# Transposes around a triangular inverse on VectorE, and head norms by one product on all rows, in a gated delta-rule layer on one core

## What is computed

```
q = l2norm(conv_silu(x Wq) + ramp * p20_q)          # the same for k; 16 heads of 16
v = conv_silu(x Wv) + ramp * p20_v
step: S = S * exp(g);  e = (v - S k) * beta;  S = S + k e^T;  o = S q * scale
reads = rmsnorm(o) over each head of 16
y = sigmoid(gate) * (concat(reads, normed_p20) @ out_W + out_b);  x1 = layernorm(x + y)
```

## Time and profile before

| what | value |
|---|---|
| median of three runs (lowest to highest) | 5939.71 us (5938.71 to 5969.02) |
| the profiled execution | 5967.04 us |
| its span, first to last instruction | 5965.4 us |
| mean granted clock of TensorE | 0.912 of full speed |
| TensorE busy in the span | 5158.8 us (86%) |
| VectorE busy | 2928.0 us (49%) |
| ScalarE busy | 1756.1 us (29%) |
| last router product of the first part starts (L1086) | 3435.3 us |

### The profile page before, as it was taken

The page is one execution under the profiler, slowest core; times in us unless marked ns, Lnnn a source line. Parts: engine busy times, 40 slices in busy tenths (PEclk is TensorE's granted clock), DMA queues, the critical chain, the costliest instruction groups (busy, mean ns, idle before and its releaser), DMA issues. The chain is left out here.

```text
span 5965.4 us, 218898 instructions
## 1 busy us (share of the span) xinstructions
PE 5158.8 (86%) x98967; PEld 3328.7 (56%) x98967; DVE 2928.0 (49%) x6701; ACT 1756.1 (29%) x2887; POOL 538.5 (9%) x657
## 2 busy tenths in 40 slices
PE   5999999999999999999999658999999999999400
PEld 3555565656656565656565535666666666666300
DVE  6667676767667676767676384000000001000255
ACT  3333333333333343434333101212212211211122
POOL 0000000000000000000000001111111111111376
PEclk9899899999999999999998679999999999999755
DMA  1000000000000000000000001111111111111365
GB/s 30 18 15 22 19 18 22 19 22 15 22 19 20 21 18 22 18 22 19 22 19 18 14 4 40 50 33 50 49 35 47 36 49 50 35 50 35 96 190 174
DMA packets 170008, 220.32 MB, mean 37 GB/s; under 512 B 32306, under 2 KB 148083, under 8 KB 169075
## 3 DMA queue, kind: packets, MB, share of 16 engines
q1 hardware_dynamic: 122994, 106.02, 5.6%
q0 software_dynamic: 29312, 84.97, 4.9%
q10 hardware_dynamic: 16896, 16.78, 0.8%
HBM read 138.50 MB, written 67.11 MB: 34 GB/s over the span
## 5 line engine op out<-in xcount | busy, mean ns | idle before, releaser
L1407 PE MATMUL bank<-gathered_T,w1s 128*128 128x512 f32 x2048 | 928.8, 613 | 67.6 <-DVE gathered_T L1350 67.6
L1418 PE MATMUL bank<-w2s,hidden_T 128*128 128x256 f32 x4096 | 894.6, 379 | 0.0
L1418 PEld LDWEIGHTS bank<-w2s,hidden_T 128*128 128x128 f32 x4096 | 775.7, 190 | 117.8 <-issue 15.3
L1377 ACT ACTIVATE hidden_T<-bank,b_expert 128x512 f32<-128x512 f32 x512 | 352.0, 687 | 1544.4 <-PE bank L1407 1544.4
L1407 PEld LDWEIGHTS bank<-gathered_T,w1s 128*128 128x128 f32 x2048 | 399.3, 196 | 559.5 <-issue 557.8
L1357 DVE TENSOR_TENSOR result_rows<-bank,b2s 128x512 f32<-128x512 f32 x128 | 88.6, 692 | 1217.7 <-PE bank L1418 1217.7
L900 PE MATMUL bank<-xT_and_z_out,ctrlW 128*128 128x512 f32 x768 | 383.9, 623 | 4.3 <-issue 4.3
L900 PE MATMUL bank<-np,p20W 128*128 128x512 f32 x768 | 375.3, 619 | 7.1 <-DVE conv_out L693 4.4
L1350 DVE COPY gathered_T<-bank 128x512 f32<-128x512 f32 x128 | 88.6, 692 | 557.8 <-PE bank L1396 541.9
L1136 POOL MEMSET tri<- 128x128 f32 x1 | 0.2, 209 | 3430.5 <-POOLq L337 3430.5
L1038 PEld LDWEIGHTS bank<-yb,bd_v 32*32 32x32 f32 x16384 | 188.7, 114 | 210.5 <-issue 209.9
(11 more groups left out here) (287 smaller groups left out, 7624.7 us busy)
## 6 DMA issues: line engine op xcount, KB each, us to landing
expert_rows<-result_rows SPq DMA_DIRECT2D x64, 512.0 KB, 2.9
x<-L_attn_hidden SPq DMA_DIRECT2D x33, 512.0 KB, 3.8
out_squares<-L_attn_hidden SPq DMA_DIRECT2D x32, 512.0 KB, 3.6
x_rows<-x SPq DMA_DIRECT2D x32, 512.0 KB, 3.1
x_rows_sb<-x_rows SPq DMA_DIRECT2D x32, 512.0 KB, 4.3
out<-out_rows ACTq DMA_DIRECT2D x32, 512.0 KB, 3.1
w1s<-L_ffn_w POOLq DMA_DIRECT2D x8, 1024.0 KB, 5.9
w2s<-L_ffn_w POOLq DMA_DIRECT2D x8, 1024.0 KB, 7.8
```

The costliest lines, as they stand in the source:

```text
L1377: nc.scalar.activation(hT[:, j, m, :], ring["h", j, m][:, :], ACT.Gelu, bias=b1e[:, par, m:m + 1]).then_inc(hT_ready, 1)
L1407: ins = nc.tensor.matmul(ps[:, :], w1s[:, par, k, m * P:(m + 1) * P], xgT[:, j, k, :], start=k == 0, stop=k == 1)
L1418: ins = nc.tensor.matmul(ps[:, i * D:(i + 1) * D], hT[:, j, m, s0:s0 + P], w2s[:, par, m, :], start=m == 0, stop=m == MT - 1)
```

## The change

**Norms.** A 128x128 matrix of ones in blocks of 16 (`hblk`) takes the place of the 128x32 sums and the 32-row spreading. One product a tile gives the head sum on all 128 rows, so ScalarE's logarithm and exponential work on all rows of each tile (into `sq4`, and `y1r` for the outputs), and VectorE scales from there. The tile `sq4` shares memory with `xT`; so the copy of the next `xT` waits for the last scaling (`kqi_ready`). The decay logits get a tile of their own (`dec_in`).

**Inverse.** VectorE transposes 32x32 blocks before and after the inverse, 512 columns an instruction, in place of TensorE and two PSUM banks. For this the first block of an eviction goes to a tile of its own, `a_rows`, with the token index outermost (an evicted group is now four VectorE instructions), and `X` has the column outermost. ScalarE reads the turned tile from SBUF.

**Order.** The four `ORDERS` strings are new. On SP's queue the log-row DMAs now stand behind the store of the unit's rows.

The diff, cut to its core:

```diff
-        X = FX[:, :].rearrange("p (h i c) -> p h i c", i=CHUNK, h=HPT // 2)
+        X = FX[:, :].rearrange("p (c b i) -> p b c i", i=CHUNK, b=4)
...
-        order += [(("nrm",), "act")] + [(("put", i), "dve") for i in range(4)]
+        order += [(("nrm", i), "act") for i in range(4)]
...
-        order += [(("aT", t), "act") for t in range(2)] + [(("T", t), "act") for t in range(2)]
...
-            pe=("CACBACCBBCCBABBABCABBABCABBACBBCCCACCACC" "ABBCACCCBBCBBACBBCBBAABBACBBAABCBAABCBAA"),
-            dve=("CBCAAACCABBABAAAABBABCBBAABCBBBBBCBBBBCB" "BBBCAABCBCCAAAAACABAAAACACACACBABBAAABBA" "AA"),
-            act=("BBACBBBBBCCAAAAAAAAABBCBABCCACCCCBBBAABB" "BACCAAACC"),
-            sp="AACC")
+            pe=("ACCABCCBCBBCBACBABBABCABBBACCACCCCACCAAC" "CACCCBBCBBABBABBABBABBACBBAABACABC"),
+            dve=("BCCAACAABCABBAAAABCBBBBAABBCABBBCABBCBBB" "CBBBABBBCBCCBBBAAAAAACAAAABBACACCAACAABB" "BAABAA"),
+            act=("BABABBCBCBCBAAACAABBAAACBCABCACCCCBBBABB" "AACABAACAACAC"),
+            sp="ACCA")
... ScalarE, streams A, B, C
+                    act.wait_ge(kqi_ready.sem, kqi_ready.before(u))
                     for e in range(2):
                         act.wait_ge(ra.filled, ra.full(u, ("xT", e)))
                         A(xT[:, e, :], ra["xT", e][:, :], ACT.Copy).then_inc(a_act, 1)
...
-                    A(rsn[:, :], ra["nrm",][:, :], ACT.Ln, scale=nsc[:, 0:1], bias=eps[:, 3:4]).then_inc(a_act, 1)
-                    A(rsn[:, :], rsn[:, :], ACT.Exp, scale=-0.5).then_inc(mrs_ready.sem, 1)
+                    for i in range(4):
+                        act.wait_ge(ra.filled, ra.full(u, ("nrm", i)))
+                        A(sq4[:, i, :], ra["nrm", i][:, :], ACT.Ln, scale=1.0 if i < 2 else float(HD),
+                          bias=eps[:, 0:1] if i < 2 else eps[:, 3:4]).then_inc(a_act, 1)
+                        for n in ((), (0,), (1,), (2, 3))[i]:
+                            act.wait_ge(a_act, ra.done(u, ("nrm", n)))
+                            A(sq4[:, n, :], sq4[:, n, :], ACT.Exp, scale=-0.5).then_inc(mrs_ready.sem, 1)
...
-                        A(X[:, :, 8 * t:8 * t + 8, :].rearrange("p h i c -> p i h c"), rb["aT", t][:, :].rearrange("p (i h c) -> p i h c", i=8, c=CHUNK),
-                          ACT.Copy, scale=-1.0).then_inc(b_act, 1)
+                        act.wait_ge(a_turned.sem, a_turned.of(u, t + 1))
+                        A(X[:, :, :, 8 * t:8 * t + 8], half(turned, t).rearrange("p (i b c) -> p b c i", b=4, c=CHUNK), ACT.Copy,
+                          scale=-1.0).then_inc(x_ready.sem, 1)
...
-                        ps = rb["T", t][:, :].rearrange("p (c g) -> p g c", g=G)
+                        act.wait_ge(t_turned.sem, t_turned.of(u, t + 1))
+                        ps = half(turned, t).rearrange("p (c g) -> p g c", g=G)
...
+                    for hh in range(2):
+                        act.wait_ge(rc.filled, rc.full(u, ("on", hh)))
+                        A(half(y1r, hh), rc["on", hh][:, :], ACT.Ln, scale=1.0 / HD, bias=eps[:, 0:1]).then_inc(c_act, 1)
+                    for hh in range(2):
+                        A(half(y1r, hh), half(y1r, hh), ACT.Exp, scale=-0.5).then_inc(ors_ready.sem, 1)
... VectorE
-                        V.tensor_tensor(apk[:, gs, 0:TILE].rearrange("p g (a i) -> p g a i", a=2), ps[:, :, 0:TILE].rearrange("p g (a i) -> p g a i", a=2),
-                                        F[:, gs, :].unsqueeze(2).broadcast_to([P, 8, 2, CHUNK]), ALU.mult)
+                        V.tensor_tensor(a_rows[:, :, gs].rearrange("p i g -> p g i"), ps[:, :, 0:CHUNK], F[:, gs, :], ALU.mult)
+                        V.tensor_tensor(apk[:, gs, 0:CHUNK], ps[:, :, CHUNK:TILE], F[:, gs, :], ALU.mult)
...
+                    for t in range(2):
+                        V.transpose(half(turned, t), a_rows[:, 8 * t:8 * t + 8, :].rearrange("p i g -> p (i g)")).then_inc(a_turned.sem, 1)
+                        yield
+                    dve.wait_ge(x_ready.sem, x_ready.of(u))
...
-                        sb_.then(V.tensor_tensor(X[:, :, j + 1:, 0:j], X[:, :, j + 1:, 0:j], t, ALU.add))
+                        sb_.then(V.tensor_tensor(X[:, :, 0:j, j + 1:], X[:, :, 0:j, j + 1:], t, ALU.add))
...
+                    for t in range(2):
+                        V.transpose(half(turned, t), half(FX, t)).then_inc(t_turned.sem, 1)
+                        yield
... TensorE
-                        ins = T.matmul(ps[PAIRS[i], :], hsum[:, :], sq4[:, i, :], start=True, stop=True)
-                        T.matmul(ps[:, :], hput[PAIRS[i], :], rsn[PAIRS[i], :], start=True, stop=True).then_inc(ra.filled, 1 + (ra.pads if i == 3 else 0))
+                        pe.wait_ge(msq_ready.sem, msq_ready.of(u, i + 1))
+                        ps = ra.take(pe, u, ("nrm", i))
+                        T.matmul(ps[:, :], hblk[:, :], sq4[:, i, :], start=True, stop=True).then_inc(ra.filled, 1 + (ra.pads if i == 3 else 0))
...
-                                ins = T.matmul(ps[r, j * G:(j + 1) * G], apk[r, :, 8 * t + j], ident[r, r], start=True, stop=True)
-                                ins = T.matmul(ps[r, j * G:(j + 1) * G], FX[r, 8 * t + j::CHUNK],
-                                               ident[r, r], start=True, stop=True)
...
+                        ps = rc.take(pe, u, ("on", hh))
+                        T.matmul(ps[:, :], hblk[:, :], half(osq, hh), start=True, stop=True).then_inc(rc.filled, 1)
```

More of the change, by code:

```diff
@@ L194, in attention @@
         FX = sb("fx", P, W2)
-        apk = sb("apk", P, G, 3 * CHUNK)
+        a_rows = sb("a_rows", P, CHUNK, G)
+        apk = sb("apk", P, G, TILE)
         bdkb = sb("bd_kb", P, G, TILE)
         tmp = sb("inverse_tmp", P, 4 * 56)
+        turned = sb("turned", P, W2)
         YB = sb("yb", P, G, TILE)
@@ L269, in attention, with ring @@
         MS = (2, 3, 0, 1, 4, 5)
-        def ring(r, order, at):
+        def ring(r, order, at, pads_by="act"):
             while len(order) % len(at):
-                order.append((("pad", len(order)), "act"))
+                order.append((("pad", len(order)), pads_by))
             return Bank(order, at, filled[r], {w: emptied[r, w] for w in ("act", "dve")})
@@ L283, in attention @@
         order += [(("mm1", t), "dve") for t in range(8)]
-        order += [(("aT", t), "act") for t in range(2)] + [(("T", t), "act") for t in range(2)]
         order += [(("Y", t), "act") for t in range(4)] + [(("M", t), "dve") for t in range(4)]
-        rb = ring("B", order, banks[3:6])
-        order = [(("L", c), "act") for c in range(NCH)] + [(("on",), "act")]
-        order += [(("put", hh), "dve") for hh in range(2)] + [(("proj", q), "dve") for q in range(2)]
+        rb = ring("B", order, banks[3:6], "dve")
+        order = [(("L", c), "act") for c in range(NCH)] + [(("on", hh), "act") for hh in range(2)]
+        order += [(("proj", q), "dve") for q in range(2)]
         order += [(("x1T", b), "act") for b in range(2)] + [(("lg",), "act")]
@@ L368, in c_ @@
                 def c_(u, k, grp, s):
-                    sp.wait_ge(rc.filled, rc.full(u, ("on",)))
+                    sp.wait_ge(rc.filled, rc.full(u, ("on", 1)))
                     rows(xres, grp, s, res_loaded.sem)
@@ L437, in a_ @@
                     yield
-                    act.wait_ge(a_dve, ra.done(u - 1, ("put", 3)))
+                    act.wait_ge(gl_ready.sem, gl_ready.before(u))
                     act.wait_ge(ra.filled, ra.full(u, ("dec",)))
@@ L769, in a_ @@
                     for i, m in enumerate(MS[0:4]):
-                        dve.wait_ge(ra.filled, ra.full(u, ("put", i)))
+                        dve.wait_ge(mrs_ready.sem, mrs_ready.of(u, i + 1))
                         if i == 0:
@@ L859, in c_ @@
                     for hh in range(2):
-                        dve.wait_ge(rc.filled, rc.full(u, ("put", hh)))
-                        V.tensor_tensor(half(oTr, hh), half(oTr, hh), rc["put", hh][:, :], ALU.mult).then_inc(c_dve, 1)
+                        dve.wait_ge(ors_ready.sem, ors_ready.of(u, hh + 1))
+                        V.tensor_tensor(half(oTr, hh), half(oTr, hh), half(y1r, hh), ALU.mult).then_inc(on_done.sem, 1)
                         yield
@@ L1047, in c_ @@
                     pe.wait_ge(osq_ready.sem, osq_ready.of(u))
-                    ps = rc.take(pe, u, ("on",))
                     for hh in range(2):
-                        ins = T.matmul(ps[PAIRS[hh], :], hsum[:, :], half(osq, hh), start=True, stop=True)
-                    ins.then_inc(rc.filled, 1)
-                    yield
-                    pe.wait_ge(ors_ready.sem, ors_ready.of(u))
-                    for hh in range(2):
-                        ps = rc.take(pe, u, ("put", hh))
-                        T.matmul(ps[:, :], hput[PAIRS[hh], :], onr[PAIRS[hh], :], start=True, stop=True).then_inc(rc.filled, 1)
+                        ps = rc.take(pe, u, ("on", hh))
```

(1 more changed line is left out.)

113 lines of the change are left out of this document (36 added, 77 removed).

## The result

The changed kernel takes 5896.06 us (median of 9 runs, 5877.39 to 5914.16), the kernel before, on the same chips, 5941.86: a ratio of 0.992 with a 95% interval of 0.990 to 0.994. That is 46 us less where 200 were forecast, and 6 us above 5890, the upper end of the range given for all cases together.

What follows compares the result with a forecast made beforehand. TensorE was taken as the bound, VectorE in the inverse stretch afterwards. 7.4 less 0.5 gave 6.9 us a unit, taken as 6.5; 30 full turns gave 195, partial turns about 5: 5940 - 200 = 5740 us, range 5640 to 5890.

Steps and rivals of the forecast that it cites:

- TensorE's work, 8.0 us a unit less: First stage: removed transposing, spreading and head-sum products, less the added wide norm products, save TensorE 8.0 us a unit.
- VectorE's work: First stage: four block transposes and one more instruction per eviction add about 4.8 us a unit on VectorE.
- the rival of stepped access throughout: Inverse: every element pays 0.67 ns, 3.0 us more a unit; gain only 2.5 to 3, 5855 us; partial gain's chance 0.16.
- The stretch around the inverse, 36.6 us: Third eviction group's products to the projection's second half: VectorE becomes the bound, 36.6 us against 44.0, 7.4 less.
- The rest of the unit, 0.5 us more: Outside the inverse stretch, TensorE's: 3.91 us of products come, 4.14 go, 0.7 of state instructions move in.
- I cost both at nothing: ScalarE's extra norm instructions, at most 8.5 us a unit, and some 3 more for six turned-tile copies: hidden, zero cost.
- without that cover: ScalarE's copies from the turned tile: if the projection didn't hide them, the last two would cost 2 x 1.06 us.
- The copy of the next x: It waits for the last key scaling, sharing a tile; for this 6.9 us a unit was taken as 6.5.
- bound by its products everywhere: Rival: TensorE stays the bound throughout, all 8.0 us a unit come, most likely 5660 us; chance 0.14.
- the log-row transfers: Four transfers behind the row store on SP's queue, before the next unit's first VectorE step: nothing, bounded by 2.5 us.
- the case for "no change": The end-of-unit chain shows as well, gain under 1 us a unit, 5910 to 5970 us; chance 0.08.
- the low-clock rival: TensorE's small waits around the inverse carry the low clock into the dense products: slower, 6120 us; chance 0.07.

Runs made afterwards that it cites:

- the own tile: Changed kernel, with ScalarE's copies of the turned inverse written to a tile of their own, no order changed: 5805.02 us, ratio 0.978 to the kernel before.
- The late convolution steps: Changed kernel with copies on their own tile, plus VectorE's third and fourth convolution steps moved behind the masked values' transposes: 5827.06 us, ratio 0.981.
- the old order: The changed kernel's instructions walked in the written order of the kernel before, removed steps dropped and new ones fitted in: 5982.82 us, ratio 1.008.
- small products twice: Changed kernel with each of the eight groups of 32 small state products of a unit issued twice: 6445 us in a single run.
- one wide, with and without the own tile: Each group of 32 small state products replaced by one wide zero-weight product: 5718.54 us with copies on their own tile, 5746 us on the changed kernel.
- four packets fewer: Changed kernel with copies on their own tile and each group of 32 small state products as one wide zero-weight product: 5718.54 us, ratio 0.964.
- wide products spread further: Changed kernel with copies on their own tile, plus a control product, the projection's second half and the residual products moved among small products: 5863.52 us, ratio 0.987.

## Why the prediction was wrong

*TensorE's work, 8.0 us a unit less:* right. Its busy time per unit fell by 96.3 - 88.5 = 7.8. The norm products, priced at 0.98, cost 134.4 / 128 = 1.05 and 64.0 / 64 = 1.00, two records to a product:
```profile
L956 PE MATMUL bank<-xT_and_z_out,head_blocks 128*128 128x512 f32 x256 | 134.4, 629 | 3.9 <-issue 3.8
...
L1028 PE MATMUL bank<-out_squares,head_blocks 128*128 128x512 f32 x128 | 64.0, 624 | 4.9 <-ACT out_squares L569 4.9
```
*VectorE's work:* the prices were right or a little off. The groups of VectorE, 0 to 3500 us:
```profile
L819 DVE TENSOR_TENSOR fx<-fx,inverse_tmp 128x56 f32<-128x56 f32 (+6 forms) x448 | 147.0, 328 | 15.3
...
L797 DVE TENSOR_TENSOR a_rows<-bank,fx 128x128 f32<-128x128 f32 x256 | 93.5, 365 | 185.3 <-PE bank L977 185.1
...
L798 DVE TENSOR_TENSOR apk<-bank,fx 128x128 f32<-128x128 f32 x256 | 68.5, 267 | 0.0
L825 DVE STREAM_TRANSPOSE turned<-fx 128x512 f32<-128x512 f32 x64 | 45.0, 704 | 0.1
```
Transposes took 0.70 (0.62 forecast), the stepped eviction 0.10 more than its unstepped neighbour (0.09 forecast). The inverse steps stand at 328 ns as before: the rival of stepped access throughout fell, and its price of 0.67 ns an element, right for the eviction, doesn't hold for short inner rows.

*The stretch around the inverse, 36.6 us:* the length is close, the reason given for it is not. The window above begins with the third group's products, which take about 0.9, so the stretch is 39.06 - 0.9 = 38.2 us in that unit; over the ten units of 1000 to 2000 us the same cut gives 35.4 to 39.5, mean 37.3, and the kernel before 44.0. With the own tile it is 37.09 - 0.9 = 36.2 in the unit that I followed (mean of ten 36.7):
```profile
1560.43:1597.52 37.09, 31.76 (x1012) 20.38 (x1011) 33.76 (x94) 17.30 (x28) 0.00 (x0) 0.95 0.06 18
```
But VectorE isn't the bound that it was forecast to be. It works 33.87 of the 39.06 us, where 36.3 in a row were added up, and waits for TensorE in the rest; TensorE's waits in the stretch are 5.3 us (mean of the ten units), as forecast, but only 1.6 of them end with VectorE, where 4 to 7 were the sign, and 2.9 are issue waits. The views of the unit shown, VectorE's wait first:
```profile
DVE state_wide L858 <- PE bank L1022: 2.9, 4, 1.2
```
```profile
PE bank L1022 <- issue: 4.4, 3, 2.2
PE bank L977 <- DVE bd_kb L800: 1.1, 2, 0.6
```
The two errors nearly cancel, so that the length came out is in part luck. The late convolution steps say the same: 2.7 us less for VectorE there gained nothing.

*The rest of the unit, 0.5 us more:* this is where the time was lost. 58.4 us were forecast; 99.7 - 37.3 = 62.4 were measured. Its busy time came about as forecast, 56.5 us; its waits grew from 1.0 to 5.8. Two steps failed.

The first is "I cost both at nothing", of ScalarE's copies from the turned tile. The cover that I named, two and a half quarters of the projection, is real. But the copies write `bd`, which VectorE's transposes of the masked values must have left, and the new order puts these last; I moved the steps without asking what each copy waits for. The six copies together took 3.1 us more than before, near the "some 3" that the bound allowed; it isn't their length that failed but where they could start. The wait itself is 1.4 us a unit. With the copies on a tile of their own it went, and 1.5 of issue waits with it: 2.9 us a unit, 91 us of the 156 missing. The bound that I kept "without that cover", 2 x 1.06 = 2.1, lies between the two.

The second is a term that the sum didn't have, TensorE's instruction supply. I gave TensorE about 5 us of waits in the stretch and left the rest of the unit at its old length, plus 0.5. The issue waits, 2.9 us a unit before, grew to 7.4. The removed products were wide or 64x64 and needed few instructions for their time, so the packets fell only from 22.4 to 21.1 a unit while the engine got 7.8 us less work to hide them behind. In the old order the same work still shows 3.8 us of issue waits and more waits on other engines; the new order closes those waits, and issue waits come in their place.

The runs that added packets (small products twice) and removed them (one wide, with and without the own tile) show that it is the supply, and in these products, as does the end of every issue wait behind a packet. Its size is known less well. With the own tile, 65 us above the forecast, issue waits are still 2.9 us a unit above those before, some 90 us in 31 units. With four packets fewer the kernel came to 5719, or 5741 without what the edit saves in product time. That this is the forecast's 5740 is chance, as no kernel that was forecast has four packets fewer; the run shows only that the supply is large enough to cover the rest.

*The copy of the next x,* for which 0.4 us a unit was taken off: TensorE has no wait on it in the view of its waits.

*The rivals:* none came. TensorE isn't bound by its products everywhere, the clock over the 1000 us is 0.94 as before, and the log-row transfers, costed at nothing, appear in none of the waits above. Nor did the case for "no change" name what happened, although the time came near it. The page that I set against the low-clock rival, "TensorE: Matmul & The Clock Gate" of the Trainium skill, Part 1, stays undecided here. The sum of waits doubled while the clock stayed at 0.94, which speaks against its rule; the small products twice, with 18.2 us of waits a unit, had 0.88, which agrees; and the old order had 0.92 with the same 11.1 us as the changed kernel.

Not settled: which of its moves cost the version with wide products spread further its 58 us, why the clock differs between orders with the same sum of waits, and how much of the 156 us each of the two failed steps takes by itself.

## What to carry to other kernels

When products are removed or packed closer, count the instructions that stay: in this kernel a small product needs as many as a large one, and once less other work and fewer other waits hide their supply, waits without a releaser appear in the middle of their groups. Before you call such a wait anything else, compare its end with the starts of the instruction packets. When a new order shortens one wait, look at the sum of all waits and at the busy time, not at that wait alone. When a step moves from one engine to another, follow each of its successors to every tile that it writes; a cover that is long enough is worth nothing if the work can't start under it. Here a tile of its own removed the wait, and putting its cause earlier only moved it to what stood there.

## What was not expected of the hardware

TensorE's instructions come in packets of 16.4 KB, one every 3.9 to 4.1 us where small products follow one another and at least 3.3 us apart all through 1000 to 3000 us, and 128 records of 32x32 products use one up, though two such groups follow one another at 0.56 us each (1530.69 to 1531.25 above). A group therefore costs 0.56 us if its instructions have come and about 2 us, half of the time between packets, if they haven't. The Trainium skill, "Runtime: NRT & Kernel Launch", section "Instruction fetch mechanics", says that instructions are refilled in blocks of 16 KiB, the next one while the current one runs, so that the cost is mostly hidden. The trace agrees on the block; that it is hidden holds for wide products, and not for these, where one more packet cost 2.1 us of issue waits and one fewer gave back 0.7 to 0.9.

A copy of 512 columns on ScalarE with stepped reads from SBUF took 1.20 us; the same copy into the same places, with its stepped reads from PSUM, took 0.67 in the kernel before:
```profile
L545 ACT ACTIVATE bd<-bank,pair_mask 128x512 f32<-128x512 f32 x64 | 42.9, 671 | 9.7 <-DVE bd_v L823 9.7
```
```profile
L550 ACT ACTIVATE bd<-turned,pair_mask 128x512 f32<-128x512 f32 x64 | 76.7, 1198 | 143.0 <-DVE bd_v L832 143.0
```
